# The attention stage of an audio tower on one core: the order of one group's work, by pairs of heads instead of single heads

## The chip, the cores and the metric

The kernel runs on one core of a Trainium2 chip. The metric is the device time of one execution in microseconds (us).

## The reference

The input is 32 clips of 375 frames with 80 features. A tokenizer turns windows of 8 frames (stride 4) into slots (93 a clip for the 375 frames of this input) with 256 features each (two dense layers with relu, then a batch normalisation). Then follow one attention layer and one mixture-of-experts layer:

```python
h = tok(x)                                   # (32, slots, 256)
h = h + attn(layernorm(h))                   # 16 heads of 64
h = h + ffn(layernorm(h))                    # a shared expert, and 2 of 8 routed ones
...
q, k, v = (einsum('bsm,hmd->bhsd', x, kernel[i]) for i in range(3))
attn = softmax(einsum('bhsd,bhtd->bhst', q, k) * scale, axis=-1)
out = einsum('bhst,bhtd->bhsd', attn, v)
out = transpose(out, (0, 2, 3, 1)).reshape(b, s, d * h)
out = einsum('bsf,fm->bsm', out, WO[0])
...
probs = softmax(einsum('bsh,he->bse', x, router_w)); top_k_prob, top_k_idx = top_k(probs, 2)
```

Everything is float32. The batch normalisation needs all clips before the attention starts.

## The kernel before

There are three stages, one after the other: the tokenizer, the attention with the router, and the experts. The change is in the second alone. It works on NG = 8 groups of GB = 4 clips (N = 372 token columns, C = 3 chunks of R = 124 rows). The 16 heads of a group are taken as NJ = 8 pairs j, and a head is called a unit u (NU = 16; unit u belongs to pair u // 2). The engines work through hand-written lists of steps, each list in its own order, and wait for each other through semaphores.

The steps of a pair on TensorE (PE):

- `qk_tile` "qj" and "kj": 6 matmuls each of 128x128 by 372 columns (line 908). Every product is made of three passes of high and low halves.
- `scores(g, j)`: 16 matmuls on 64 rows of the array (line 921). The two heads sit on the upper and the lower 64 rows and run side by side.
- `turn(g, u)`: 4 transposes of the unit's scaled probabilities (line 929) into the one bank t_ps.
- `values(g, j)`: 16 matmuls (line 942) that fill 64 columns of the array each. The two heads sit on different columns and run side by side.
- `output(g, j)`: 9 matmuls into y_ps (line 954).
- `v_tile`: 6 matmuls by 512 columns (line 894), 8 such tiles a group.

Between these stand the single steps of the neighbouring groups: `rows_tile` "p10" and "p11" (the next group's rows, line 626), `back_tile` "z20", "z21" (the last group's normalised rows, turned for the router) and "z10", "z11" (the next group's, turned for its projections; line 634), `logits_tile` (lines 644, 646) and `rank_tile` (lines 655, 657).

All tiles named q, k, v, p, z, logits and rank pass through two banks of pj_ps, bank 0 and bank 1, each in a fixed order. `begin` makes TensorE wait until the tile before in the same bank has been taken out. ScalarE (ACT) takes q, k, p10, p11 and the v tiles of bank 0; VectorE (DVE) takes the v tiles of bank 1, the logits and the ranks. A z tile is taken by both: ACT writes the high half (`hi`), then DVE the low half (`lo`), and only then is the bank free. k, p11 and the v tiles with an odd last digit are in bank 1, the rest in bank 0, and z tiles go by their last digit.

The chain of a unit: `scores` (PE), `shift` (DVE: maximum, line 1164, and subtraction, line 1167), `exps` (ACT, line 1063), `total` (DVE: sum, line 1173, and reciprocal, line 1175), the scaling (GpSimd, line 1301), `turn` (PE), `take_turned` (ACT, line 1069), `values` (PE), `take_o` (ACT high half, line 1074, then DVE low half, line 1179), `output` (PE). prob and probT have four slots each, u % 4.

Before, each list went over 16 slots s, one unit a slot. On TensorE an even slot held scores, both projections, an output, a v tile where the table V has one, turn(s - 2) and values, and an odd slot a v tile and turn(s - 2). So values stood between the two turns of a pair, and the odd unit's turn ahead of the next scores. DVE interleaved one shift with one total, and ran the router's steps (`route`: max, shift, sum, recip, scale, top, index, expert, masks, both, rank, pick, slots) in small portions between them. The first group has no group behind it and the last none ahead; groups 2 to 6 run in a loop with register counters. After the last group comes `drain`, and beside it the shared expert's weights are split (`shared_hi` on ACT, `shared_lo` on DVE).

Of the kernel before, what the change touches and what calls it, by code (L numbers as in the profile page):

```python
# [79 lines left out]
def audio_tower_kernel(nc, x, W1, b1, W2, b2, gamma, beta, qkv_w, WO, sh_up, sh_down, rt_up, rt_down, router_w, out):  # L80
# [8 lines left out]
    MC = HD // P  # L89
# [25 lines left out]
    with ExitStack() as ctx:  # L115
# [416 lines left out]
        with ExitStack() as c:  # L532
# [353 lines left out]
            def _(pe):  # L886
# [73 lines left out]
                def group(g, behind, ahead):  # L960
                    V = {0: "v00", 1: "v01", 2: "v02", 3: "v03", 5: "v10", 7: "v11", 9: "v12", 11: "v13"}
                    for s in range(NU):
                        if s > 0 and s % 2 == 0:
                            scores(g, s // 2)
                        if s % 2 == 0 and s // 2 + 1 < NJ:
                            qk_tile(g, "q%d" % (s // 2 + 1))
                            if s == 0:
                                scores(g, 0)
                            qk_tile(g, "k%d" % (s // 2 + 1))
                        if s % 2 == 0 and s >= 6:  # L970
                            output(g, s // 2 - 3)
                        elif s % 2 == 0 and behind:
                            output(g - 1, NJ + s // 2 - 3)
                        if s == 10 and behind:
                            logits_tile(pe, g, g - 1)
                        if s == 14 and ahead:
                            qk_tile(g, "q0")
                        if s in V:
                            v_tile(g, V[s])
                        if s == NU - 1 and behind:  # L980
                            rank_tile(pe, g, g - 1)
                        if s >= 2:
                            turn(g, s - 2)
                        elif behind:
                            turn(g - 1, NU + s - 2)
                        if s == NU - 1 and ahead:
                            qk_tile(g, "k0")
                        if s in (1, 2) and ahead:
                            rows_tile(pe, g, s - 1, g + 1)
                        if s == 9 and behind:  # L990
                            back_tile(pe, g, 1, 1, g - 1, x_rows)
                            back_tile(pe, g, 1, 0, g - 1, x_rows)
                        if s == 13 and ahead:
                            back_tile(pe, g, 0, 0, g + 1, z_rows)
                            back_tile(pe, g, 0, 1, g + 1, z_rows)
                        if s % 2 == 0 and s >= 4:
                            values(g, s // 2 - 2)
                        elif s % 2 == 0 and behind:
                            values(g - 1, NJ + s // 2 - 2)
# [18 lines left out]
                def drain():  # L1018
                    g = NG - 1
                    output(g, NJ - 3)  # L1020
# [10 lines left out]
            def _(act):  # L1031
# [44 lines left out]
                def group(g, behind, ahead):  # L1076
                    V = {0: "00", 2: "02", 5: "10", 9: "12"}
                    for s in range(NU):
                        if s % 2 == 0 and s // 2 + 1 < NJ:
# [838 lines left out]
```

## Time and profile before

| | |
|---|---|
| median of 3 runs | 1072.42 us (1072.33 to 1073.98) |
| the profiled execution, its own time | 1070.59 us |
| its span in the profile | 1069.0 us |
| TensorE matmul busy | 1018.5 us, 95% of the span |
| VectorE, ScalarE, GpSimd busy | 621.9, 507.6, 426.1 us |
| attention stage on TensorE | from 103.8 us (first scores) to 609.4 us |

The busy time of TensorE is the union of modelled intervals, so two starts in a row tell more of its pace than its busy share. In a timeline a row is a block of equal instructions: start, length, engine, line, operation, tiles, count, and in brackets the idle time ahead of it with what ended it.

### The profile page before, as it was taken

Reading aid. Unit: us, or ns where it says so; the run is one execution under the profiler, and the core shown is the slowest. Engines: PE = TensorE matmul, PEld = TensorE weight load, DVE = VectorE, ACT = ScalarE, POOL = GpSimd, SP = SyncE. Lnnn points to the kernel's source line nnn. Section 1 sums busy time; section 2 is a strip of 40 time slices with the busy share of each in tenths; the row PEclk is TensorE's granted clock in tenths of the full one; section 3 lists DMA queues with packets and bytes.
Section 4 is the critical chain, followed back from the end, with each engine's and each line's share of the span. In section 5 each row is a group of like instructions: output and inputs, shape, how many; then the busy total and the mean of one; then the engine's idle time right before and its main releaser. Section 6 shows DMA issues by size and latency. Waiting matters only on the chain. (4 is left out here: it accounts for less than half of the span.)

```text
span 1069.0 us, 24219 instructions
## 1 busy us (share of the span) xinstructions
PE 1018.5 (95%) x8364; PEld 948.6 (89%) x8365; DVE 621.9 (58%) x1610; ACT 507.6 (47%) x1129; POOL 426.1 (40%) x535
## 2 busy tenths in 40 slices
PE   5995999999999999999999799999999999999998
PEld 5994798888888888888888699999999999999998
DVE  3665666767777676877757655433443343363565
ACT  3552554444544445454444464444555454454352
POOL 2001231445253443525343250606661626543885
PEclk9997999999999999999999699999999999999999
DMA  9615999900010100001011153331443134411555
GB/s 185 140 42 196 362 345 344 330 15 17 29 29 29 24 33 14 14 29 29 29 25 45 53 158 99 103 136 60 138 137 123 58 128 133 137 51 43 163 155 137
DMA packets 104628, 115.32 MB, mean 108 GB/s; under 512 B 29856, under 2 KB 94848, under 8 KB 104576
## 3 DMA queue, kind: packets, MB, share of 16 engines
q1 hardware_dynamic: 75936, 73.82, 22.6%
q0 software_dynamic: 18176, 29.12, 9.4%
q10 hardware_dynamic: 10464, 11.70, 3.3%
q8 instruction: 31, 0.51, 0.2%
q14 instruction: 21, 0.17, 0.0%
HBM read 51.53 MB, written 62.95 MB: 107 GB/s over the span
## 5 line engine op out<-in xcount | busy, mean ns | idle before, releaser
L1301 POOL TENSOR_TENSOR prob<-prob,rc 93x372 f32<-93x372 f32 x128 | 102.9, 804 | 294.4 <-DVE rc L1175 293.9
L1856 DVE TENSOR_TENSOR act_s<-up_ps,act_s 128x384 fp32r<-128x384 f32 (+1 forms) x168 | 81.7, 493 | 176.6 <-ACT up_ps L1703 175.3
L908 PE MATMUL pj_ps<-xg,wA 128*128 128x372 f32 x768 | 151.5, 344 | 5.4 <-DVE split L744 2.7
L1701 ACT ACTIVATE act_s<-up_ps 128x384 fp32r<-128x384 f32 (+1 forms) x168 | 73.7, 439 | 148.8 <-PE up_ps L1594 144.3
L908 PEld LDWEIGHTS pj_ps<-xg,wA 128*128 128x128 f32 x768 | 128.8, 190 | 13.3 <-DVE split L744 3.8
L894 PE MATMUL pj_ps<-wB,xg 128*93 128x512 f32 x384 | 102.6, 403 | 0.8 <-ACT h_s L666 0.8
L1069 ACT ACTIVATE probT<-t_ps 93x372 f32<-93x372 f32 x128 | 60.5, 473 | 83.7 <-PE t_ps L929 83.3
L1594 PE MATMUL up_ps<-rx,wB 128*128 128x256 f32 (+1 forms) x576 | 86.4, 308 | 0.7 <-issue 0.7
L1179 DVE TENSOR_TENSOR oT<-o_ps,oT 128x372 fp32r<-128x372 f32 x64 | 34.8, 543 | 89.3 <-ACT oT L1074 88.3
L1608 PE MATMUL dn_ps<-wB,act_s 128*128 128x256 f32 x720 | 85.5, 279 | 0.0
L1594 PEld LDWEIGHTS up_ps<-rx,wB 128*128 128x128 f32 x576 | 83.6, 188 | 1.6 <-issue 0.9
L954 PE MATMUL y_ps<-wB,oT 128*124 128x256 f32 x576 | 81.7, 287 | 2.3 <-DVE oT L1179 2.3
L1608 PEld LDWEIGHTS dn_ps<-wB,act_s 128*128 128x128 f32 x720 | 83.4, 188 | 0.0
L1164 DVE TENSOR_REDUCE mx<-s_ps 93x4 f32<-93x372 f32 x128 | 67.2, 525 | 22.7 <-PE s_ps L921 22.4
L954 PEld LDWEIGHTS y_ps<-wB,oT 128*124 128x124 f32 x576 | 76.8, 189 | 3.5 <-DVE oT L1179 2.7
L894 PEld LDWEIGHTS pj_ps<-wB,xg 128*93 128x93 f32 x384 | 56.6, 158 | 25.3 <-ACT h_s L666 2.0
L1490 POOL DMA_INDIRECT raw<-y_rows,y_at x48 | 62.6, 1305 | 31.6 <-issue 31.0
L1703 ACT ACTIVATE up_ps<-up_ps 128x384 f32<-128x384 f32 (+1 forms) x168 | 71.2, 424 | 5.3
L1167 DVE TENSOR_TENSOR prob<-s_ps,mx 93x372 f32<-93x372 f32 x128 | 69.4, 542 | 7.5
L929 PEld LDWEIGHTS t_ps<-ident,prob 93*93 93x93 f32 x512 | 59.3, 163 | 16.2 <-issue 6.2
L929 PE MATMUL t_ps<-ident,prob 93*93 93x93 f32 x512 | 65.2, 250 | 4.9 <-POOL prob L1301 4.8
L1173 DVE TENSOR_REDUCE sm<-prob 93x4 f32<-93x372 f32 x128 | 67.5, 527 | 4.0 <-ACT prob L1063 4.0
(201 smaller groups left out, 1958.7 us busy)
## 6 DMA issues: line engine op xcount, KB each, us to landing
slots<-zeros SPq DMA_DIRECT2D x8, 3072.0 KB, 23.3
y_rows<-zeros SPq DMA_DIRECT2D x5, 2688.0 KB, 20.0
rows_in<-slots SPq DMA_DIRECT2D x22, 384.0 KB, 3.5
y_rows<-rows_out ACTq DMA_DIRECT2D x22, 384.0 KB, 2.5
raw<-in_L_ffn_routed_up POOLq DMA_DIRECT2D x7, 1024.0 KB, 5.4
raw<-in_L_ffn_routed_down POOLq DMA_DIRECT2D x7, 1024.0 KB, 8.2
ln_out<-split SPq DMA_DIRECT2D x8, 744.0 KB
frames<-in_x SPq DMA_DIRECT2D x8, 400.0 KB
```

What stands on the lines that cost most here:

```text
L894: ins = pe.matmul(pj_ps[0:TP, b % 2, 0:VW], xg[:, dp, m, b * TP:(b + 1) * TP], wB[:, wp, at:at + VW], start=(k == 0), stop=(k == 5))
L908: ins = pe.matmul(pj_ps[:, t, 0:N], wA[:, wp, at:at + P], xg[:, dp, m, :], start=(k == 0), stop=(k == 5))
L929: ins = pe.transpose(t_ps[:, i * TP:(i + 1) * TP], prob[:, u % 4, i, :], ident[0:TP, 0:TP])
L954: ins = pe.matmul(y_ps[0:R, c // 2, c % 2 * HD:(c % 2 + 1) * HD], oT[:, j % 2, dp, c * R:(c + 1) * R], wB[:, wp, at:at + HD], start=(j == ...
L1167: dve.tensor_tensor(prob[:, u % 4, :, 0:SL], s4, mx[:, u % 2, :].unsqueeze(2).broadcast_to([TP, 4, SL]), ALU.subtract).then_inc(shifted, 1)
L1173: dve.tensor_reduce(sm[:, u % 2, :], prob[:, u % 4, :, 0:SL], AX, ALU.add).then_inc(sum_done, 1)
L1301: pool.tensor_tensor(p, p, rc[:, u % 2, :].unsqueeze(2).broadcast_to([TP, 4, SL]), ALU.mult).then_inc(scaled, 1)
L1594: ins = pe.matmul(up_ps[:, f % 4, 0:width], w[:, wp, at:at + P], rx[:, dp, m, 0:width], start=(k == 0), stop=(k == 5))
L1608: ins = pe.matmul(dn_ps[:, a // 2, a % 2 * HD:(a % 2 + 1) * HD], act_s[:, dp, f, a * P:(a + 1) * P], w[:, wp, at:at + HD], start=(k == 0), ...
L1701: act.activation(act_s[:, HI, f, 0:width], up_ps[:, f % 4, 0:width], ACT.Gelu).then_inc(ract_hi, 1)
L1703: act.activation(up_ps[:, f % 4, 0:width], up_ps[:, f % 4, 0:width], ACT.Gelu).then_inc(rgelu_done, 1)
L1856: dve.tensor_tensor(act_s[:, LO, f, 0:width], up_ps[:, f % 4, 0:width], act_s[:, HI, f, 0:width], ALU.subtract).then_inc(ract_lo, 1)
```

## The change

Every list now goes over 8 pairs p. On TensorE a pair is: scores(p), q of the next pair, the turn of the odd unit 2p - 3, k of the next pair, output(p - 3), the v tile of slot 2p, the turn of the even unit 2p - 2, the v tile of slot 2p + 1, values(p - 2), and then straight the next pair's scores. In pair 0 q1 still stands ahead of the scores. The single steps keep their pair, with other neighbours: p11 is directly ahead of v03, z21 and z20 directly behind v12, z10 and z11 behind turn(10), rank behind q0 and turn(12). ACT follows: exps(2p) behind the first taken projection and turn, exps(2p + 1) behind k and behind the v tile of slot 2p; normalise_batch stands at the head of pair 0. DVE does both shifts, then both totals; total(15) comes inside the group; all the router's steps but the rank's stand ahead of take_o, in pair 6 too, where take_o(4) is the last. In the last group the shared weights' splitting goes by pairs, with the third portion on ACT directly ahead of the drain. No instruction is added or taken away, and no buffer changes.

Lines taken out are those of the functions printed above and are left out here, but for one.

```diff
--- before.py
+++ after.py
@@ -959,44 +959,53 @@
 
 def group(g, behind, ahead):
     V = {0: "v00", 1: "v01", 2: "v02", 3: "v03", 5: "v10", 7: "v11", 9: "v12", 11: "v13"}
...
+    for p in range(NJ):
+        if p > 0:
+            scores(g, p)
+        if p + 1 < NJ:
+            qk_tile(g, "q%d" % (p + 1))
+            if p == 0:
                 scores(g, 0)
...
+        if p >= 2:
+            turn(g, 2 * p - 3)
+        elif behind:
+            turn(g - 1, NU + 2 * p - 3)
+        if p + 1 < NJ:
+            qk_tile(g, "k%d" % (p + 1))
+        if p >= 3:
+            output(g, p - 3)
+        elif behind:
+            output(g - 1, NJ + p - 3)
+        if p == 5 and behind:
             logits_tile(pe, g, g - 1)
...
+        if p == NJ - 1 and ahead:
             qk_tile(g, "q0")
...
+        if 2 * p in V:
+            v_tile(g, V[2 * p])
+        if p >= 1:
+            turn(g, 2 * p - 2)
+        elif behind:
+            turn(g - 1, NU - 2)
+        if p == 1 and ahead:
+            rows_tile(pe, g, 1, g + 1)
+        if 2 * p + 1 in V:
+            v_tile(g, V[2 * p + 1])
+        if p == NJ - 1 and behind:
             rank_tile(pe, g, g - 1)
...
+        if p == NJ - 1 and ahead:
             qk_tile(g, "k0")
...
+        if p == 0 and ahead:
+            rows_tile(pe, g, 0, g + 1)
+        if p == 4 and behind:
             back_tile(pe, g, 1, 1, g - 1, x_rows)
             back_tile(pe, g, 1, 0, g - 1, x_rows)
...
+        if p == 6 and ahead:
             back_tile(pe, g, 0, 0, g + 1, z_rows)
             back_tile(pe, g, 0, 1, g + 1, z_rows)
...
+        if p >= 2:
+            values(g, p - 2)
+        elif behind:
+            values(g - 1, NJ + p - 2)
 
 def start():
     rows_tile(pe, -1, 0, 0)
@@ -1017,6 +1026,7 @@
 
 def drain():
     g = NG - 1
+    turn(g, NU - 3)
     output(g, NJ - 3)
     turn(g, NU - 2)
     values(g, NJ - 2)
@@ -1075,41 +1085,51 @@
 
 def group(g, behind, ahead):
     V = {0: "00", 2: "02", 5: "10", 9: "12"}
...
+    for p in range(NJ):
+        if p == 0 and ahead:
+            normalise_batch(g + 1)
+        if p + 1 < NJ:
+            take_q(g, p + 1, g)
+        if p >= 2:
+            take_turned(g, 2 * p - 3)
+        elif behind:
+            take_turned(g - 1, NU + 2 * p - 3)
+        exps(g, 2 * p)
+        if p + 1 < NJ:
+            take_k(g, p + 1, g)
+        if p == NJ - 1 and ahead:
             take_q(g, 0, g + 1)
...
+        if 2 * p in V:
+            take_v(g, "v" + V[2 * p])
+        exps(g, 2 * p + 1)
+        if p >= 1:
+            take_turned(g, 2 * p - 2)
         elif behind:
...
+            take_turned(g - 1, NU - 2)
+        if p == 1 and ahead:
+            take_rows(act, g, 1, g + 1)
+        if 2 * p + 1 in V:
+            take_v(g, "v" + V[2 * p + 1])
+        if p == NJ - 1 and ahead:
             take_k(g, 0, g + 1)
...
+        if p == 0 and ahead:
+            take_rows(act, g, 0, g + 1)
+        if p == 4 and behind:
             hi(act, g, 1, 1, g - 1)
             hi(act, g, 1, 0, g - 1)
...
+        if p == 6 and ahead:
             hi(act, g, 0, 0, g + 1)
             hi(act, g, 0, 1, g + 1)
...
+        if p >= 2:
+            take_o(g, p - 2)
+        elif behind:
+            take_o(g - 1, NJ + p - 2)
+        if p == 5 and behind:
+            exp_logits(act, g - 1)
+        if not ahead and p >= 6:
+            shared_hi(p - 6)
+    if not ahead:
+        shared_hi(2)
 
 def shared_hi(q):
 
@@ -1131,6 +1151,7 @@
 
 def drain():
     g = NG - 1
+    take_turned(g, NU - 3)
     take_turned(g, NU - 2)
     take_o(g, NJ - 2)
     shared_hi(3)
@@ -1178,69 +1199,57 @@
     dve.wait_ge(o_hi, g * NJ + (j + 1))
     dve.tensor_tensor(oT[:, j % 2, LO, :], o_ps[:, 0:N], oT[:, j % 2, HI, :], ALU.subtract).then_inc(o_lo, 1)
 
...
+def routing(n, steps):
+
+    for step in steps.split():
         route(dve, n, step)
 
 def group(g, behind, ahead):
     V = {1: "01", 3: "03", 7: "11", 11: "13"}
...
+    for p in range(NJ):
+        shift(g, 2 * p)
+        shift(g, 2 * p + 1)
+        total(g, 2 * p)
         if behind:
...
+            if p == 4:
+                normalise(dve, g, 1, g - 1, x_rows)
+            if p == 5:
+                keep(dve, g - 1, x_rows)
+                handed(dve, g)
+            if p == 6:
+                routing(g - 1, "sum recip scale top")
+        total(g, 2 * p + 1)
+        if p == 2 and behind:
+            add(g - 1)
+            moments(dve, g, 1, g - 1)
+            spread(dve, 1, g - 1)
+        if p == 1 and ahead:
+            moments(dve, g, 0, g + 1)
+            spread(dve, 0, g + 1)
+        if p == 5 and behind:
+            take_logits(dve, g, g - 1)
+            routing(g - 1, "max shift")
+        if 2 * p + 1 in V:
+            take_v(g, "v" + V[2 * p + 1])
+        if p == 5 and ahead:
+            normalise(dve, g, 0, g + 1, z_rows)
+        if p == 4 and behind:
+            for m in reversed(range(MC)):
+                lo(dve, g, 1, m, g - 1)
+        if p == 6 and ahead:
             lo(dve, g, 0, 0, g + 1)
             lo(dve, g, 0, 1, g + 1)
...
+        if p == 6 and behind:
+            routing(g - 1, "index expert masks both")
+        if p == NJ - 1 and behind:
+            take_ranks(dve, g, g - 1)
+            routing(g - 1, "pick slots")
+        if p >= 2:
+            take_o(g, p - 2)
+        elif behind:
+            take_o(g - 1, NJ + p - 2)
+        if not ahead and p >= 6:
+            shared_lo(p - 6)
 
 def shared_lo(q):
 
@@ -1281,7 +1290,6 @@
 
 def drain():
     g = NG - 1
-                    total(g, NU - 1)
     take_o(g, NJ - 2)
     shared_lo(2)
     shared_lo(3)
```

## Rows read from the trace of the kernel before

**Rows 1.** Who waited for whom, one middle group (217.4 to 280.2 us): total, times, longest.

```profile
PE pj_ps L908 <- DVE split L744: 0.4, 1, 0.4
```

**Rows 2.** Timeline of TensorE, one regular pair of a middle group.

```profile
308.37 0.90 PE L921 MATMUL s_ps<-kT,qT 64*93 64x93 f32 x16
309.20 2.30 PE L908 MATMUL pj_ps<-xg,wA 128*128 128x372 f32 x12
311.34 1.23 PE L954 MATMUL y_ps<-wB,oT 128*124 128x256 f32 x9
312.42 0.49 PE L929 MATMUL t_ps<-ident,prob 93*93 93x93 f32 x4
312.84 0.87 PE L942 MATMUL o_ps<-probT,v_rows 93*64 93x93 f32 x16
313.63 1.62 PE L894 MATMUL pj_ps<-wB,xg 128*93 128x512 f32 x6
315.09 0.49 PE L929 MATMUL t_ps<-ident,prob 93*93 93x93 f32 x4
```

**Rows 3.** Timeline of TensorE in the first group, around tile p11 (line 626).

```profile
113.12 1.54 PE L894 MATMUL pj_ps<-wB,xg 128*93 128x512 f32 x6
114.50 0.49 PE L929 MATMUL t_ps<-ident,prob 93*93 93x93 f32 x4
114.82 0.39 PE L626 MATMUL pj_ps<-ident,hs 128*124 128x128 f32 x2
115.98 1.60 PE L894 MATMUL pj_ps<-wB,xg 128*93 128x512 f32 x6 [0.77 <-ACT h_s L666]
```

**Rows 4.** Timeline of ScalarE, the same place: v02 and p11 taken.

```profile
114.69 0.59 ACT L1051 ACTIVATE v_rows<-pj_ps 93x512 f32<-93x512 f32 x1 [0.90 <-PE pj_ps L894]
...
115.55 0.38 ACT L666 ACTIVATE h_s<-pj_ps 124x256 f32<-124x256 f32 x1
```

**Rows 5.** Timeline of TensorE behind v12 (slot 9), with tiles z21 and z20 (line 634).

```profile
383.61 1.61 PE L894 MATMUL pj_ps<-wB,xg 128*93 128x512 f32 x6
...
385.38 1.06 PE L634 MATMUL pj_ps<-ident,x_rows 124*128 124x124 f32 x6
386.37 0.90 PE L921 MATMUL s_ps<-kT,qT 64*93 64x93 f32 x16
387.67 0.95 PE L908 MATMUL pj_ps<-xg,wA 128*128 128x372 f32 x4 [0.40 <-DVE split L744]
```

**Rows 6.** Timeline of TensorE from a group's rank tile into the next group: k0, then q1.

```profile
343.18 0.47 PE L657 MATMUL pj_ps<-both,ones_w 124*124 124x24 f32 x3
343.89 0.54 PE L929 MATMUL t_ps<-ident,prob 93*93 93x93 f32 x4 [0.24 <-POOL prob L1301]
344.21 1.27 PE L908 MATMUL pj_ps<-xg,wA 128*128 128x372 f32 x6
345.74 1.29 PE L908 MATMUL pj_ps<-xg,wA 128*128 128x372 f32 x6 [0.26 <-DVE next_row L821]
```

**Rows 7.** Timeline of VectorE, slots 11 to 14 of a middle group.

```profile
332.94 0.69 DVE L1151 COPY v_rows<-pj_ps 93x512 f32<-93x512 f32 x1
...
334.51 0.54 DVE L1164 TENSOR_REDUCE mx<-s_ps 93x4 f32<-93x372 f32 x1
...
335.55 0.16 DVE L778 TENSOR_REDUCE row_sum<-ex 124x3 f32<-124x24 f32 x1
...
340.91 0.16 DVE L789 COPY p_q<-tops 124x6 f32 x1
...
342.12 0.53 DVE L1173 TENSOR_REDUCE sm<-prob 93x4 f32<-93x372 f32 x1
```

**Rows 8.** Timeline of all engines, the stage's end: the last pair's scores and the last addition.

```profile
589.24 0.90 PE L921 MATMUL s_ps<-kT,qT 64*93 64x93 f32 x16
...
609.44 1.02 DVE L1158 TENSOR_TENSOR h_s<-h_s,y_ps 124x512 f32<-124x512 f32 x2 [2.37 <-PE y_ps L954]
```

**Rows 9.** Windows: per stretch, busy us (count) of PE, PEld, DVE, ACT, POOL, then granted clock.

```profile
596.00:598.00 2.00, 1.02 (x9) 0.81 (x7) 1.90 (x8) 1.65 (x3) 0.21 (x1) 0.78 0.00 0
```

More of the change, by code:

```diff
@@ L1091, in group @@
                             take_k(g, 0, g + 1)
-                        if s in (1, 2) and ahead:
-                            take_rows(act, g, s - 1, g + 1)
-                        if s == 9 and behind:
+                        if p == 0 and ahead:
+                            take_rows(act, g, 0, g + 1)
+                        if p == 4 and behind:
                             hi(act, g, 1, 1, g - 1)
                             hi(act, g, 1, 0, g - 1)
-                        if s == 13 and ahead:
+                        if p == 6 and ahead:
@@ L1098, in group @@
                             hi(act, g, 0, 0, g + 1)
                             hi(act, g, 0, 1, g + 1)
-                        exps(g, s)
-                        if s % 2 == 0 and s >= 4:
-                            take_o(g, s // 2 - 2)
-                        elif s % 2 == 0 and behind:
-                            take_o(g - 1, NJ + s // 2 - 2)
-                        if ahead:
-                            if s == 0:
-                                normalise_batch(g + 1)
-                        if behind:
-                            if s == 11:
-                                exp_logits(act, g - 1)
@@ L1111, in group @@
-                        if not ahead and s >= 13:
-                            shared_hi(s - 13)
+                        if p >= 2:
[8 more added lines that the diff above has]
+                        shared_hi(2)
@@ L1179, in take_o @@
                     dve.tensor_tensor(oT[:, j % 2, LO, :], o_ps[:, 0:N], oT[:, j % 2, HI, :], ALU.subtract).then_inc(o_lo, 1)
-                def routing(s, place, n):
-                    plan = {11: ("max", "shift", ""), 12: ("sum", "recip", "scale top"), 13: ("", "", "index expert masks both"),
-                            15: ("", "", "pick slots")}
-                    for step in plan.get(s, ("", "", ""))[place].split():
+                def routing(n, steps):
+                    for step in steps.split():
                         route(dve, n, step)
@@ L1209, in group @@
                             lo(dve, g, 0, 0, g + 1)
                             lo(dve, g, 0, 1, g + 1)
-                        if s in V:
-                            take_v(g, "v" + V[s])
-                        if behind:
-                            if s == 8:
-                                normalise(dve, g, 1, g - 1, x_rows)
-                            if s == 10:
-                                keep(dve, g - 1, x_rows)
-                        if s % 2 == 0 and s >= 4:
-                            take_o(g, s // 2 - 2)
-                        elif s % 2 == 0 and behind:
-                            take_o(g - 1, NJ + s // 2 - 2)
@@ L1242, in group @@
-                        if not ahead and s >= 14:
-                            shared_lo(s - 14)
+                        if p == 6 and behind:
[7 more added lines that the diff above has]
+                            take_o(g - 1, NJ + p - 2)
```

78 lines of the change are left out of this document (removed).

## The prediction

> **What bounds the kernel now.** I read the page first: TensorE's matmuls are busy for 95% of the span, and no other engine is above 58%. The list of waits, taken over one middle group, then says how much of TensorE's time is waiting at all. The reader is to see how short it is: the row of the z tiles, 0.4 us in a group of 62.8 us, is one of the two longest of TensorE [rows 1]. So the stage is bound by TensorE's own list, and a change of order can win only in two places: in what TensorE loses between blocks of different shape, and in the few waits. It can lose by making new waits. All three are read from the starts of blocks in the timeline of TensorE, since the busy time counts a modelled length that overlaps the next block.
>
> **Changes of shape.** Scores use half of the rows of the array for a head, values half of the columns, all else the whole. Four transposes ahead of another whole-array block take 0.32 us (114.50 to 114.82), but 0.42 ahead of values (312.42 to 312.84) [rows 2, 3]. A v tile takes 1.38 behind a projection (113.12 to 114.50) and 1.46 behind values (313.63 to 315.09) [rows 2, 3]. So entering a half-array block costs about 0.09 in the block before and, by the second pair of its matmuls starting later, some 0.05 to 0.07 within; leaving costs 0.08 within the next block and about 0.10 at the end of its own. A regular pair before changes shape four times: turn to values, values to v tile, turn to scores, scores to projection. After, values stand directly ahead of scores, and there are three changes. What that one change costs, no row shows. Bounds: 0, if two half-array blocks follow each other as if alike; 0.34, if it costs a way out and a way in (0.10 + 0.08 and 0.09 + 0.07). I take 0.17, one change, since the weights of one shape must leave for the other as at every other change, and once. That saves 0.17, less some 0.03 because a projection behind a turn starts a little later than one behind its like (an estimate: k0 takes 1.10 without its wait, where 6 of the 12 projections of [rows 2] take 1.07). Values meet scores in pairs 1 to 7 of groups 1 to 7 and pairs 3 to 7 of the first: 54 times. 54 x 0.135 = **7.3 us saved**.
>
> The Trainium skill has a rule here (TensorEngine Tiling (Array Packing), Key Properties): a change of tiling mode drains the engine, a change of tile within a mode doesn't. By it values to scores, columns halved to rows halved, is still a change of mode and costs one drain, as I took it; were it only another tile, the saving would be 7 us larger. The trace agrees so far as each change it has costs something; the new one it doesn't show.
>
> **Old waits that go.** I follow each tile that TensorE waited for into the new lists.
> - q1 of the next group waited for the rank's taking, on DVE behind two shifts. k0 starts 344.21 and q1 345.74: 1.53 for 1.10, and q1's own start costs 0.11 more. Ahead of it turn(13) started 0.71 behind a block of 0.33, 0.38 late [rows 6]. Now turn(13) is behind the next scores, and between rank and q1 stand k0 and values. About 0.9, 6 times: 5.4.
> - q6 waited for z20's low half: it starts 1.30 behind scores of 0.83, 0.47 late [rows 5]. Now values and scores are between (1.65 us, and the taking needs 1.30 from z20's end): 7 times, 3.3.
> - p10 waited for normalise_batch, now at the pair's head: 0.28 in six groups and 1.03 in the first: 2.7. In the last group turn(1) waited 0.8 for GpSimd and now stands 2 us later. z20's old wait for v12's taking is 0.19 to 0.28, 7 times: 1.4 (its successor is below). v03's, 0.3 in all.
> Together **13.9 us**.
>
> **New waits.** Times count from a pair's scores; q starts at 0.83, the odd turn 1.95, k 2.25, output 3.3, the even turn 4.4, then v tiles, values, next pair [rows 2].
> - v03 directly behind p11, same bank. The first group already has just this, since it has no values to put between: p11's two transposes need 0.22, but v03 starts at 115.98, 1.16 behind 114.82, so 0.93 of waiting [rows 3]. ScalarE takes v02 at 114.69, then a turn, then p11, done 115.93 [rows 4]. The new list puts exps(3), some 0.4, behind take_v too, so 1.33, and 0.06 for a start after standing still. Six groups at 1.39, and 0.40 more in the first: 8.7. On ScalarE, only take_o(7) is behind it, and waits for PE anyway.
> - z20 behind v12, now without a turn between. v12 is taken 2.23 us from its start (2.29 in the old place), and z20 is reached after 1.39 + 0.33: 0.51, 7 times: 3.6 [rows 5].
> - output(4) in pair 7 needs take_o(4), now DVE's last step of pair 6. DVE's list from v13, which is filled 7.6 us into pair 5 (8.28 long): copy and normalise 1.57 (332.94 to 334.51), take_o(3) 0.46, two shifts of 1.04 (334.51 to 335.55) [rows 7]. That ends at 3.4 of pair 6. Then total 0.66 (0.53 and a short step), four router steps 0.94 (estimates from the short steps of some 0.2), total 0.66, two lo of 0.46, then index to both 1.21 (340.91 to 342.12) [rows 7], take_o 0.54: ready at 8.5. Pair 6 is 6.26 long and TensorE reaches output at 1.2 of pair 7, which is 7.45. Late by 1.05 to 1.15, and 0.1 for the start. 6 x 1.2 = 7.4 (the last group's is counted with the tail). Behind that output wait q0, rank and k0; behind take_o on DVE are shift(14) and (15), which have 5 us of room.
> - rank needs q0's bank. Only turn(12), 0.33, is between now, where values were too; q0's taking comes 0.8 behind its end: 0.48, 6 times: 2.9.
> Together **22.6 us**. DMA issues on GpSimd keep their units, and those on SP wait for the z tiles' splitting, which stays in its pair; take_o(0), behind the additions and moments on DVE, is ready at 2.1 of pair 3, and its output comes at 3.3.
>
> **The tail.** From the last scores to the last addition it takes 20.2 us (589.24 to 609.44) [rows 8], and the granted clock falls on the way from 2.4 towards 1.2 GHz, to a mean of 0.78 in the stretch where TensorE is busy for 1.02 of 2 us [rows 9]; it had stood still for about 3 of the last 4 us. In the new order output(5) waits for a take_o(5) behind the last pick and slots, and comes 1.9 us later (8.3 against 6.4 from the last scores). The steps after it then run closer together. Worked through at full clock the tail would take 16.5, at half clock from output(5) on 21.5. The stillness ahead of output(5) is about as long as before (3.4 us), so I lean to the low clock: from -3.7 to +1.3, taken as **+0.5**.
>
> **The sum.** -7.3 - 13.9 + 22.6 + 0.5 = +1.9, say 2.0 us. The profiled execution's own time is 1070.59 (span 1069.0, 1.6 us around it), 1.8 below the median; against it the sum gives 1072.6, against the median 1074.4. Differences under 0.2%, 2.1 us, are about what a measurement of this kernel can't tell from none, so this stands on the border between no change and slower.
>
> **Rivals.**
> - *The change of shape is free between values and scores.* Another 0.17 at 54 places, of which the two ahead of output(4) are lost in its wait: -7, 1067.4. For it: both kinds run two heads side by side. Against it: every change in [rows 2] costs.
> - *DVE is ready for output(4).* If its list between v13 and take_o(4) takes 1.1 us less than the sum of its steps, 7.4 us go: 1067.0. Against it: my figures are starts to starts, and in the old trace those steps run without gaps.
> - *The tail keeps its clock.* -4.2 against my value: 1070.2. It decides at whether TensorE's stillness ahead of output(5) is short enough.
> - *Clearly slower: DVE falls behind one step more.* DVE's list in pairs 5 to 7 is full; each 1 us that it starts later, for instance when the shifts of pair 6 wait for turn(9) or a router step is slower than 0.2, comes out at output(4) in full, 7 times: at +0.8 each it is +6, 1080. The same price has a change of values to scores that costs 0.34 instead of 0.17. It decides from 0.3 us on.
>
> **Chances.** The forecast, new waits a little larger than what is saved, 0.55, with a range of its own from 1071.5 to 1077.5: of it 0.02 below, 0.25 within and 0.28 above. The free change 0.12, the ready DVE 0.12, both faster. The tail at full clock 0.08, within 0.2% by itself. Clearly slower 0.13. So faster 0.26, the same 0.33, slower 0.41. The range from 1067 to 1080 takes in the first faster cases at its edge and the slower one; a chance of 0.2 is left for two rivals at once.
>
> **What would show it.** Right: in a middle group's timeline scores start 0.17 behind the last of values; v03 starts 1.5 us behind p11; z20 half a us late; output(4) waits for DVE's oT, about 1 us in every group but the first; turn(13), q1 and q6 start without waits; DVE shows take_o(4) behind the router's mask sums. The group gets longer, from 62.8 to about 63.4 us. Wrong: output(4) or v03 without a wait, or a new wait of TensorE that I haven't named, above all ahead of scores or a turn; or a tail that isn't within 16 to 22 us.

## The result, and the profile after

The changed kernel takes 1076.99 us, median of 6 runs (1075.07 to 1077.60), where the kernel before took 1072.43 (1072.33 to 1073.98) in 6 runs on the same chip. The ratio is 1.0036, 95% interval 1.0026 to 1.0046, so it is slower by 3.9 us (2.8 to 4.9). The forecast was 1074.4 in a range from 1067 to 1080, with slower as the likeliest side at 0.41. The profiled execution, the fastest of the six, took 1075.07 (span 1073.5), 4.5 more than the profiled one of before.

The split of that time stands in one view: the windows of one middle group, from one rank tile to the next. The columns are the stretch and its length, the busy time and instructions of TensorE, its weight loads, VectorE, ScalarE and GpSimd, then the granted clock, the DMA share and GB/s. The kernel before:

```profile
343.06:405.89 62.83, 61.78 (x573) 53.86 (x571) 45.24 (x135) 30.36 (x69) 26.49 (x49) 1.00 0.08 24
```

and the changed kernel:

```profile
345.22:409.15 63.93, 60.80 (x570) 52.74 (x571) 47.94 (x134) 30.84 (x70) 26.39 (x49) 1.00 0.08 24
```

TensorE's busy time falls by 0.98 us a group; I put that down to the change of shape and to more closely packed blocks. Its idle time rises from 1.05 to 3.13. The group is 1.10 longer. VectorE's busy time, for the same list of instructions, rises by 2.7. Short products of 124x24 elements make 1.0 of that: in this group `scale` takes 616 ns instead of 173, and the two of `pick` take 430 each on average instead of 161.

Where TensorE stands still, its timeline in the changed kernel shows. The end of pair 6 and pair 7 of a middle group:

```profile
339.56 0.90 PE L921 MATMUL s_ps<-kT,qT 64*93 64x93 f32 x16
340.39 0.57 PE L929 MATMUL t_ps<-ident,prob 93*93 93x93 f32 x4
342.22 1.33 PE L954 MATMUL y_ps<-wB,oT 128*124 128x256 f32 x9 [1.27 <-DVE oT L1200]
...
344.41 0.49 PE L929 MATMUL t_ps<-ident,prob 93*93 93x93 f32 x4
345.22 0.28 PE L655 MATMUL pj_ps<-both,before_w 124*124 124x32 f32 x1 [0.32 <-ACT qT L1049]
...
346.86 0.87 PE L942 MATMUL o_ps<-probT,v_rows 93*64 93x93 f32 x16
347.66 1.28 PE L908 MATMUL pj_ps<-xg,wA 128*128 128x372 f32 x6
```

The output starts 1.83 behind a turn that is followed after 0.40 where nothing is waited for (e7 below): 1.43 late. Rank starts 0.81 behind the turn and not 0.33: 0.48. And q1, the last row, starts 0.80 behind values, at once: the old wait [rows 6] is gone. The tiles p11 and v03, same view:

```profile
362.77 0.39 PE L626 MATMUL pj_ps<-ident,hs 128*124 128x128 f32 x2
364.32 1.63 PE L894 MATMUL pj_ps<-wB,xg 128*93 128x512 f32 x6 [1.17 <-ACT h_s L666]
```

v03 comes 1.55 behind a tile of 0.22: 1.33 late, in all seven groups that have it, 0.40 more than in the first group of before [rows 3]. The z tiles behind v12:

```profile
386.84 0.48 PE L634 MATMUL pj_ps<-ident,x_rows 124*128 124x124 f32 x3
387.68 0.54 PE L634 MATMUL pj_ps<-ident,x_rows 124*128 124x124 f32 x3 [0.36 <-ACT v_rows L1061]
388.15 0.87 PE L942 MATMUL o_ps<-probT,v_rows 93*64 93x93 f32 x16
388.95 0.90 PE L921 MATMUL s_ps<-kT,qT 64*93 64x93 f32 x16
```

z20 starts 0.84 behind z21, which alone takes 0.32, so it is 0.52 late. The last two rows are values and the next scores, 0.80 apart. A regular pair now takes 7.04 or 6.99 us, from scores to scores, where it took 7.14 [rows 2]. Last, the tail:

```profile
592.67 0.90 PE L921 MATMUL s_ps<-kT,qT 64*93 64x93 f32 x16
...
599.23 0.57 PE L929 MATMUL t_ps<-ident,prob 93*93 93x93 f32 x4 [1.42 <-ACT probT L1079]
601.78 2.28 PE L954 MATMUL y_ps<-wB,oT 128*124 128x256 f32 x9 [1.99 <-DVE oT L1200]
```

From the last scores to the last addition (613.53, line 1179 of the changed kernel) it takes 20.9 us, where it took 20.2 [rows 8]. The last scores themselves come 3.4 us later than before.

### The profile page after: what moved, and what is told of

Read it like the earlier page. It is cut to its first block and busy times, and to the rows that moved or that the text cites. A ratio compares the mean times of both kernels' runs of the same rounds, so it can differ in the third digit from the quotient of the medians.

```text
span 1073.5 us, 24219 instructions
## 1 busy us (share of the span) xinstructions
PE 1011.0 (94%) x8364; PEld 940.5 (88%) x8365; DVE 639.7 (60%) x1610; ACT 510.5 (48%) x1129; POOL 425.8 (40%) x535
## 5 line engine op out<-in xcount | busy, mean ns | idle before, releaser
L1309 POOL TENSOR_TENSOR prob<-prob,rc 93x372 f32<-93x372 f32 x128 | 107.3, 839 | 286.0 <-DVE rc L1196 284.9
L908 PE MATMUL pj_ps<-xg,wA 128*128 128x372 f32 x768 | 163.9, 350 | 1.0 <-DVE xg L744 1.0
L1049 ACT ACTIVATE qT<-pj_ps 128x372 f32<-128x372 f32 x64 | 30.7, 480 | 88.3 <-PE pj_ps L908 88.3
L1073 ACT ACTIVATE prob<-prob 93x372 f32<-93x372 f32 x128 | 64.8, 506 | 16.3 <-DVE prob L1188 15.7
L838 POOL DMA_INDIRECT slots<-x_rows,slot_now x42 | 55.8, 1329 | 29.2 <-issue 29.2
```

The costliest lines, as they stand in the source:

```text
L908: ins = pe.matmul(pj_ps[:, t, 0:N], wA[:, wp, at:at + P], xg[:, dp, m, :], start=(k == 0), stop=(k == 5))
L1309: pool.tensor_tensor(p, p, rc[:, u % 2, :].unsqueeze(2).broadcast_to([TP, 4, SL]), ALU.mult).then_inc(scaled, 1)
```

## The experiments

The theory: the new order gains what the prediction said, and four new waits of TensorE, each the place of one tile behind another, eat more than that; each can be taken away by an exchange of neighbours. The rivals: the waits only move to the next step; VectorE is too full to be ready anywhere; or the time is lost through the clock. Differences to the changed kernel are worked out from the two ratios to before, times 1072.5 us. The interval of one ratio is 1 us to either side (2 us for e3, e6, e7 and e11), so e4 and e6 aren't told from the changed kernel by their times alone. The last column is read from the profiled executions: the time from the first scores to the last, against the changed kernel's 488.8 us. It leaves out the tail, whose clock differs from one execution to the next: with the changed kernel's order there, it took 22.2 us from the last scores to the next stage in the changed kernel and 20.3 (e5) to 23.5 (e1) in the others.

| | median us | ratio to before (95%) | against the changed kernel | trace, first to last scores |
|---|---|---|---|---|
| changed kernel | 1076.99 | 1.0036 (1.0026 to 1.0046) | | (before: +3.3) |
| e1_take_o_first | 1071.37 | 0.9993 (0.9983 to 1.0003) | -4.6 | -6.4 |
| e2_p11_ahead | 1071.01 | 0.9985 (0.9976 to 0.9995) | -5.5 | -6.1 |
| e3_values_between | 1079.27 | 1.0063 (1.0045 to 1.0081) | +2.9 | +2.7 |
| e4_exps_behind | 1074.78 | 1.0026 (1.0016 to 1.0035) | -1.1 | -2.8 |
| e5_v12_ahead | 1070.77 | 0.9988 (0.9978 to 0.9998) | -5.1 | -4.3 |
| e6_values_ahead_rank | 1074.91 | 1.0026 (1.0008 to 1.0045) | -1.1 | +2.5 |
| e7_all_waits | 1048.76 | 0.9774 (0.9755 to 0.9793) | -28.1 | -25.1 |
| e8_scale_early | 1074.09 | 1.0016 (1.0006 to 1.0025) | -2.1 | -2.2 |
| e9_tail | 1071.05 | 0.9986 (0.9976 to 0.9995) | -5.4 | 0.0 |
| e10_before_normalise | 1070.13 | 0.9976 (0.9967 to 0.9986) | (before: -2.6) | (before: -2.8) |
| e11_turn_between | 1056.46 | 0.9858 (0.9839 to 0.9878) | (e7: +9.0) | (e7: +10.0) |

**e1_take_o_first: output(4)'s wait.** On VectorE, pair 6, take_o goes ahead of four router steps.

```diff
-            if p == 6 and behind:
-                routing(g - 1, "index expert masks both")
             if p >= 2:
                 take_o(g, p - 2)
             elif behind:
                 take_o(g - 1, NJ + p - 2)
+            if p == 6 and behind:
+                routing(g - 1, "index expert masks both")
```

> Against the changed kernel (1077.0 us), VectorE takes o of pair 4 ahead of the four router steps index to both, in pair 6, and does nothing else otherwise. Theory: output(4) waits 1.43 us a group because those 1.21 us of steps stand ahead of take_o(4), behind a list that is full since v13; without them the wait is under 0.2, the rank's masks are still in time, and 6 groups give 7 to 8 us: about 1069. Rival: the wait is ScalarE's high half of o or the scores' shifts, and the order on VectorE doesn't matter: 1077, the wait stays over 1 us.

Measured: 1071.37. Timeline of TensorE, same place:

```profile
340.20 1.34 PE L954 MATMUL y_ps<-wB,oT 128*124 128x256 f32 x9
...
342.40 0.49 PE L929 MATMUL t_ps<-ident,prob 93*93 93x93 f32 x4
343.35 0.28 PE L655 MATMUL pj_ps<-both,before_w 124*124 124x32 f32 x1 [0.45 <-ACT qT L1049]
...
594.48 0.94 PE L929 MATMUL t_ps<-ident,prob 93*93 93x93 f32 x4 [2.85 <-ACT probT L1079]
```

The output's wait is gone but for 0.2. A middle group is 62.86, 1.07 less, and the last rank tile comes 6.2 us earlier (590.24 against 596.43; 7.5 counted from the first scores of either). The step behind the output takes 0.13 a group back, rank's own wait being 0.62 instead of 0.49. From the last rank tile to the next stage 2.4 more are lost: the turn behind that tile's values now waits 2.85 for ScalarE where it waited 1.42, and the granted clock is low from 592.9 on, where it was low from 600.8. Which of the two is the cause of the other is not shown. The place is shown, and so is that a microsecond won there isn't wholly won at the end.

**e8_scale_early: why that wait was 0.3 longer than forecast.** The router's first four steps stand ahead of both totals instead of between them.

```diff
             shift(g, 2 * p + 1)
+            if p == 6 and behind:
+                routing(g - 1, "sum recip scale top")
             total(g, 2 * p)
             if behind:
...
-                if p == 6:
-                    routing(g - 1, "sum recip scale top")
             total(g, 2 * p + 1)
```

> Against the changed kernel, the four router steps sum, recip, scale and top stand ahead of both totals in pair 6 instead of between them. The same work, 0.94 to 1.4 us, stays ahead of take_o(4). In the changed kernel scale takes 0.61 us and runs beside GpSimd's scaling of unit 12, in the kernel before 0.17 and beside nothing. Theory: scale is held up while GpSimd works, and here it takes 0.17 again, so that output(4) waits 0.44 less, 6 x 0.44 = 2.6: about 1074.4. Rival: its length comes from something else (the operands, the record); it stays 0.61 and the time 1077.

The reason for it is in the timeline of GpSimd and VectorE of the changed kernel, pair 6:

```profile
337.63 0.80 POOL L1309 TENSOR_TENSOR prob<-prob,rc 93x372 f32<-93x372 f32 x1 [5.96 <-DVE rc L1196]
337.65 0.18 DVE L780 RECIPROCAL row_sum<-row_sum 124x3 f32<-124x3 f32 x1
337.86 0.61 DVE L782 TENSOR_TENSOR ex<-ex,row_sum 124x24 f32<-124x24 f32 x1
338.63 0.30 DVE L786 MAX8 tops<-ex 124x8 f32<-124x8 f32 x3 [0.15 <-DVE ex L782]
```

The `scale` step, a product of 124x24 elements, starts 0.23 behind the start of GpSimd's scaling and ends 0.04 behind its end (338.47 and 338.43). Its median over the eight groups is 615 ns, in the kernel before 173. The reciprocal one row up, which has one input, also ran beside GpSimd and took its usual 0.18. The experiment, same step and then the output that waits:

```profile
337.45 0.18 DVE L782 TENSOR_TENSOR ex<-ex,row_sum 124x24 f32<-124x24 f32 x1
...
342.21 1.33 PE L954 MATMUL y_ps<-wB,oT 128*124 128x256 f32 x9 [0.90 <-DVE oT L1200]
```

The wait falls from 1.27 to 0.90 and the group by 0.36; 1074.09, 2.1 less, where 2.6 was expected. So total(12), by starting GpSimd, held up `scale`, which stood behind it on VectorE. The Trainium skill (SBUF — State Buffer, Who interferes with whom) has the rule: a VectorE instruction with two inputs in SBUF contends with a GpSimd instruction that reads SBUF, and the second to start is blocked until the first is done. The trace agrees to 0.04 us at the end of `scale`; whether it was held from its first element isn't shown, and spans on GpSimd are rough.

**e2_p11_ahead and e4_exps_behind: v03's wait.** e2 moves p11 (and its taking on ScalarE) from directly ahead of v03 to ahead of v02. e4 leaves TensorE alone and moves exps(3) on ScalarE from ahead of p11's taking to behind it.

```diff
 # e2, TensorE; ScalarE's take_rows likewise
+            if p == 1 and ahead:
+                rows_tile(pe, g, 1, g + 1)
             if 2 * p in V:
                 v_tile(g, V[2 * p])
...
-            if p == 1 and ahead:
-                rows_tile(pe, g, 1, g + 1)
 # e4, ScalarE
-            exps(g, 2 * p + 1)
+            if p != 1:
+                exps(g, 2 * p + 1)
...
             if p == 1 and ahead:
                 take_rows(act, g, 1, g + 1)
+            if p == 1:
+                exps(g, 2 * p + 1)
```

> Against the changed kernel, tile p11 and its taking stand ahead of v02 instead of ahead of v03; no bank order changes. Theory: v03's wait of 1.33 us in seven groups is the chain take v02, exps, take turned, take p11 on ScalarE, and goes entirely; p11 itself finds k2 taken. 7 x 1.4 = 9.5 us: about 1067.5. Rival: bank 1 is then short between k2 and p11 and the wait moves ahead by half: 1072.

> Against the changed kernel (1077.0 us), exps(3) stands behind the taking of p11 on ScalarE instead of ahead of it, so that the chain v02, turn, p11 is what it was in the kernel before. Theory: v03's wait of 1.33 us falls to the 0.93 that the first group had before; 0.4 in seven groups, 2.8 us: about 1074.2. Rival: the wait is set by v02's taking alone and stays 1.33: 1077.

e2 gives 1071.01, 5.5 less where 9.5 was expected (6.1 in the trace). v03's wait is gone (pair 1 is 8.60 long, not 10.02), but k3 has one that was not there:

```profile
302.06 0.49 PE L929 MATMUL t_ps<-ident,prob 93*93 93x93 f32 x4
302.79 1.29 PE L908 MATMUL pj_ps<-xg,wA 128*128 128x372 f32 x6 [0.24 <-DVE v_rows L1172]
```

It starts 0.73 behind the turn instead of 0.28. It needs v03's bank, and VectorE takes v03 only behind `moments` and `spread`. The group is 0.93 shorter: 1.33 less 0.45, within 0.05. Here the rival of the moved wait is right, for a third of the gain. In e4 v03 is still late, but less:

```profile
361.48 0.39 PE L626 MATMUL pj_ps<-ident,hs 128*124 128x128 f32 x2
362.64 1.63 PE L894 MATMUL pj_ps<-wB,xg 128*93 128x512 f32 x6 [0.77 <-ACT h_s L666]
```

0.77 of idle time for 1.17: the exponential's 0.40, as the prediction had put it into this wait. The group is 63.54, 0.39 less. The time is 1.1 less by the ratios and 2.2 by the medians, where 2.8 was expected; the trace up to the last scores is 2.8 shorter.

**e5_v12_ahead: z20's wait.** v12, and its taking on ScalarE, go ahead of output(1) in pair 4.

```diff
+            if p == 4:
+                v_tile(g, V[9])
             if p >= 3:
                 output(g, p - 3)
...
-            if 2 * p + 1 in V:
+            if 2 * p + 1 in V and p != 4:
                 v_tile(g, V[2 * p + 1])
```

> Against the changed kernel (1077.0 us), v12 stands ahead of output(1) in pair 4, so that an output and a turn lie between it and z21, z20. Theory: z20 waits 0.52 us in seven groups for ScalarE's taking of v12 alone, and this goes: 3.6 us, about 1073.4. Rival: z20 waits for the z21 half's taking or for the normalised rows, and stays: 1077.

```profile
383.14 1.54 PE L894 MATMUL pj_ps<-wB,xg 128*93 128x512 f32 x6
384.51 1.24 PE L954 MATMUL y_ps<-wB,oT 128*124 128x256 f32 x9
385.59 0.49 PE L929 MATMUL t_ps<-ident,prob 93*93 93x93 f32 x4
385.92 0.80 PE L634 MATMUL pj_ps<-ident,x_rows 124*128 124x124 f32 x6
```

The six transposes of both z tiles stand in one block: no wait. The group is 0.59 shorter for a wait of 0.52. Up to the last scores the trace is 4.3 shorter. The time is 5.1 less, 1.5 more than expected; in the profiled execution the clock was also low for less of the tail, which took 20.3 us to the next stage instead of 22.2.

**e6_values_ahead_rank: rank's wait.** values(5) goes ahead of rank in pair 7.

```diff
+            if p == NJ - 1:
+                values(g, p - 2)
             if p == NJ - 1 and behind:
                 rank_tile(pe, g, g - 1)
...
-            if p >= 2:
+            if 2 <= p < NJ - 1:
                 values(g, p - 2)
+            elif p >= 2:
+                pass
```

> Against the changed kernel, values of pair 5 stand ahead of the rank tile in pair 7, and k0 behind it. No meeting of values and scores is lost, since q1 follows either way. Theory: the rank's wait of 0.49 us for q0's taking goes and q1 finds the ranks taken, 6 x 0.49 = 2.9 us: about 1074.1. Rival: VectorE takes the ranks too late for q1, which is now only k0 behind, and the wait comes back as in the kernel before: 1077.

1074.91, but with runs from 1071.37 to 1079.82, far more apart than those of the others. The profiled one is the slowest. In it the one group between rank tiles in which the clock stays takes 63.35, 0.58 less than 63.93 for a wait of 0.49. In four groups it takes 64.87 to 64.89. There the windows and the timeline of TensorE show:

```profile
340.00:344.50 4.50, 3.73 (x16) 3.73 (x17) 3.28 (x9) 0.52 (x2) 0.80 (x1) 0.62 0.00 0
```

```profile
338.92 0.57 PE L929 MATMUL t_ps<-ident,prob 93*93 93x93 f32 x4
340.77 2.12 PE L954 MATMUL y_ps<-wB,oT 128*124 128x256 f32 x9 [1.28 <-DVE oT L1204]
342.69 1.97 PE L908 MATMUL pj_ps<-xg,wA 128*128 128x372 f32 x6
```

Behind the wait for take_o(4), 1.28 us of idle time, output takes 2.12 us and the projection 1.97, where they took 1.33 and 1.18. The granted clock is 0.62 over these 4.5 us, between its levels of 1.2 and 2.4 GHz, and that costs 1.5. So the exchange takes the rank's wait away, and a wait that was left standing beside it became dearer. By its times alone e6 shows no clear gain.

**e9_tail: the order in the last group.** VectorE's first portion of the shared weights goes behind the last shifts, totals and ranks, take_o(5) ahead of the ranks, and ScalarE's third portion behind the first turn of the drain.

```diff
 # VectorE
+            if p == NJ - 1 and not ahead:
+                take_o(g, p - 2)
             if p == NJ - 1 and behind:
                 take_ranks(dve, g, g - 1)
                 routing(g - 1, "pick slots")
-            if p >= 2:
+            if p == NJ - 1 and not ahead:
+                shared_lo(0)
+            elif p >= 2:
                 take_o(g, p - 2)
...
-            if not ahead and p >= 6:
-                shared_lo(p - 6)
+            if p == NJ - 1 and not ahead:
+                shared_lo(1)
 # ScalarE
-    if not ahead:
-        shared_hi(2)
...
     take_turned(g, NU - 3)
+    shared_hi(2)
     take_turned(g, NU - 2)
```

> Against the changed kernel, in the last group alone: VectorE's splitting of the shared weights' first quarter stands behind the last shifts and sums, its take_o of pair 5 ahead of the ranks, and ScalarE's third quarter behind a turn in the drain. Theory: output(5) comes some 2 us earlier, TensorE stands still less ahead of it, and the stage's end moves by 2 to 5 us, the more the later the clock falls: about 1073.5. Rival: the end is set by the last unit's chain from its scores on, whatever stands ahead: 1077.

1071.05, 5.4 less. The windows of the tail, changed kernel:

```profile
600.00:612.00 12.00, 8.93 (x58) 7.80 (x58) 5.97 (x11) 4.55 (x8) 0.57 (x1) 0.57 0.01 1
```

and e9, with the output that waits:

```profile
600.00:612.00 12.00, 8.53 (x79) 7.66 (x78) 9.26 (x20) 6.39 (x11) 1.61 (x2) 1.00 0.16 56
```

```profile
598.87 1.33 PE L954 MATMUL y_ps<-wB,oT 128*124 128x256 f32 x9 [0.38 <-DVE oT L1199]
```

output(5) starts 6.4 us behind the last scores instead of 9.1, and the granted clock is 1.00 through the whole tail, where from 600 to 612 it was 0.57. The next stage begins at 608.75 instead of 614.87, so the window of e9 has 3.25 us of it, and its counts don't compare with those of the changed kernel. The clock isn't safe in this order: in the profile of e7 (below), whose tail has it too, the first turn of the drain waits 1.34 us for ScalarE instead of 0.29, the granted clock then falls to 0.50, and from the last scores to the next stage it takes 20.5 us (568.05 to 588.58) instead of 16.3.

**e3_values_between: what values ahead of scores is worth.** The changed kernel with values ahead of the v tile in pairs 2 and 3, which takes the direct meeting away at two places of a group.

```diff
+            if p in (2, 3):
+                values(g, p - 2)
             if 2 * p + 1 in V:
                 v_tile(g, V[2 * p + 1])
...
-            if p >= 2:
+            if p >= 4:
                 values(g, p - 2)
+            elif p >= 2:
+                pass
```

> Against the changed kernel, values stand ahead of the v tile in pairs 2 and 3 of each group, so that they don't meet the scores there: 16 places with four changes of shape again instead of three. Theory: a change of shape costs some 0.17 us wherever it is, so each of these pairs is 0.14 to 0.17 us longer: 2.2 to 2.7 us, about 1079.4. Rivals: the meeting of values and scores saves nothing and only the order of waits counts: 1077.0, pairs as long as before; or the change costs 0.34: 5.4 more, 1082.

```profile
372.46 0.87 PE L942 MATMUL o_ps<-probT,v_rows 93*64 93x93 f32 x16
373.26 1.63 PE L894 MATMUL pj_ps<-wB,xg 128*93 128x512 f32 x6
374.82 0.90 PE L921 MATMUL s_ps<-kT,qT 64*93 64x93 f32 x16
```

The pair is 7.19 long instead of 7.04 and the group 0.33 longer: 0.165 a place. The time is 2.9 longer, the trace up to the last scores 2.7.

**e7_all_waits: all of them together.** e1, e2, e5, e6, e8 and e9 in one kernel, and the taking of v03 on VectorE ahead of `moments`, against the wait that e2 had uncovered.

```diff
+            if p == 1:
+                take_v(g, "v03")
             if p == 1 and ahead:
                 moments(dve, g, 0, g + 1)
...
-            if 2 * p + 1 in V:
+            if 2 * p + 1 in V and p != 1:
                 take_v(g, "v" + V[2 * p + 1])
```

> All together on the changed kernel: p11 ahead of v02 (with v03 taken ahead of the moments on VectorE, which in the run with p11 ahead alone had left 0.40 us of waiting at k3), v12 ahead of output(1), values ahead of the rank, take_o(4) ahead of index to both, scale ahead of the totals, and the tail's order. Theory: the new waits are all that was wrong with the change, they add up, and the gain of three changes of shape instead of four and of the old waits stays: 3.8 us less a middle group (60.2 against 63.9), 22.6 for six, 2 in the first and last, 3 in the tail: about 1050, faster than both kernels. Rival: with the waits gone VectorE, busy for most of a group, is the next bound, and half comes back as waits for it: 1062.

1048.76 us, ratio 0.9774 to before. Its windows for one middle group, and pair 7 in the timeline of TensorE:

```profile
334.14:394.10 59.96, 59.96 (x572) 52.86 (x570) 46.83 (x135) 30.72 (x70) 26.32 (x48) 1.00 0.09 26
```

```profile
329.51 0.90 PE L921 MATMUL s_ps<-kT,qT 64*93 64x93 f32 x16
330.34 0.57 PE L929 MATMUL t_ps<-ident,prob 93*93 93x93 f32 x4
330.74 1.32 PE L954 MATMUL y_ps<-wB,oT 128*124 128x256 f32 x9
...
333.35 0.87 PE L942 MATMUL o_ps<-probT,v_rows 93*64 93x93 f32 x16
334.14 0.28 PE L655 MATMUL pj_ps<-both,before_w 124*124 124x32 f32 x1
```

TensorE is busy for 59.96 of 59.96 us. The steps that waited for 1.43 and 0.49 stand without a gap. The rival that VectorE is too full falls with this: it does the same work, 46.83 us of it, and is in time everywhere.

**e11_turn_between: the gain of the order itself.** e7 with the even unit's turn, and its taking, behind values in pairs 0 to 6, so that values no longer meet scores, at 54 places.

```diff
-            if p >= 1:
+            if p == NJ - 1:
                 turn(g, 2 * p - 2)
...
             elif behind:
                 values(g - 1, NJ + p - 2)
+            if 1 <= p < NJ - 1:
+                turn(g, 2 * p - 2)
+            elif p == 0 and behind:
+                turn(g - 1, NU - 2)
```

> Against the version with all waits mended (1048.8 us), the even unit's turn, and its taking on ScalarE, stand behind values instead of ahead of them, in pairs 0 to 6. So values and scores meet nowhere any more, 54 places, and nothing else of the order changes. Theory: each place costs one change of shape, 0.165 us: 8.9 us, about 1057.7; a middle group goes from 59.96 to some 61.1. Rival: the meeting is worth little, and the mended version is fast for its waits alone: 1049 to 1051. Other rival: the turn is now too near the next pair's odd turn, through ScalarE and the one bank, and TensorE waits there: over 1062.

```profile
332.45 0.87 PE L942 MATMUL o_ps<-probT,v_rows 93*64 93x93 f32 x16
333.25 0.57 PE L929 MATMUL t_ps<-ident,prob 93*93 93x93 f32 x4
333.74 0.90 PE L921 MATMUL s_ps<-kT,qT 64*93 64x93 f32 x16
...
376.79 1.23 PE L954 MATMUL y_ps<-wB,oT 128*124 128x256 f32 x9
378.14 0.85 PE L634 MATMUL pj_ps<-ident,x_rows 124*128 124x124 f32 x6
```

1056.46: 9.0 us more than e7 by the ratios, 7.7 by the medians. Up to the last scores the trace is 10.0 longer (473.7 against 463.7), and the tail is shorter, with a higher clock. The group is 1.38 longer. In the first rows the turn takes 0.49 up to the scores, where it takes 0.28 between two whole-array blocks. The last two rows show that not all of it is the change of shape: z21 starts 1.35 behind the output, where it starts 1.08 behind it in the second group, which has no wait there. It waits for the normalised rows, which VectorE finishes at 378.01, and no longer has a turn ahead of it. TensorE stands still ahead of z21 for 1.8 us in six groups together. Without that 8.2 us are left, 0.15 a place.

**e10_before_normalise: one old wait.** The kernel before, with only normalise_batch moved to the head of ScalarE's group.

```diff
 # ScalarE, kernel before
+    if ahead:
+        normalise_batch(g + 1)
     for s in range(NU):
```

> The kernel before (1072.4 us) with one part of the change alone: ScalarE's normalise_batch at the head of a group instead of at the end of its first slot. Theory: p10's wait goes, 1.03 us in the first group and 0.28 in six: 2.7 us, about 1069.7. Rival: the two instructions, 1.27 us, now hold up q1 and k1 and with them the next scores, and it comes out the same: 1072.4.

1070.13, 2.6 less than before for an expected 2.7. In the first group p10 has no idle time ahead of it, where it had 0.88:

```profile
109.31 0.60 PE L626 MATMUL pj_ps<-ident,hs 128*124 128x128 f32 x4
```

The middle group is 62.52, 0.31 less. This is a gain of the change that doesn't need its order.

## Why the prediction was right

**The change of shape** (-7.3). Taken as one change of 0.17 between values and scores, so that 0.135 a place is saved. The two regular pairs show it directly, 7.04 and 6.99 for 7.14: 0.10 and 0.15. Taken back, it costs 0.165 a place in e3 and 0.15 in e11. With the free change 0.3 a place would be saved, with the dear one nothing, so both rivals fall.

**The old waits** (-13.9). None of turn(13), q1, q6, p10 and turn(1) waits any longer. e10 prices one of them by itself, p10's, 2.6 for 2.7. The others are priced with the change of shape together: for a middle group the prediction's terms are 0.95 for seven changes of shape and 0.9, 0.47, 0.28, some 0.2 for z20 and 0.04 for v03, in all 2.84. e7, which has all of these gains and none of the new waits, has a group 2.87 shorter than before (59.96 and 62.83).

**The new waits** (+22.6). All four are where they were said, and the list of TensorE's waits over a middle group names no other: v03 1.33 (forecast 1.33 and 0.06 for the start), z20 0.52 (0.51), rank 0.49 (0.48). The term that was mis-sized is output(4): 1.43, where 1.05 to 1.15 and 0.1 for the start had been forecast, so 8.6 us instead of 7.4. The step is "four router steps 0.94": it priced them by short steps that ran alone, but the new order puts them behind a total, which starts GpSimd, and one took 0.61 instead of 0.17. e8 shows it. The rival "clearly slower" had named a slower router step, at +0.8; it came at +0.2 to +0.3.

**The tail** (+0.5). To the first matmul of the next stage it takes 22.2 us (592.67 to 614.87) instead of 21.5 (589.24 to 610.78), so +0.7. The clock fell as before, and TensorE stood still for 3.4 us ahead of output(5), as forecast. That the term came out so close is partly luck: output(5) came 9.1 us behind the last scores and not 8.3, and against that the clock was up again before the last output, which took 1.32 instead of 2.28. The five other runs of the changed kernel, with mean clocks of 0.981 to 0.986 for this one's 0.987, took 1.2 to 2.5 us longer; how their tails went isn't traced. e9 shows that another order can keep the clock: 16.3 us to the next stage (from 592.50), a gain of 5.9 on the changed kernel. e7 shows that this order doesn't always, and what decides it isn't settled.

**The sum.** +1.9 was forecast. With what was measured for the new waits (23.5) and the tail it is -7.3 - 13.9 + 23.5 + 0.7 = +3.0. The ratio says +3.9 (2.8 to 4.9), the profiles +4.5, of which 4.0 are in the attention stage. About 1.0 of what is beyond lies ahead of the tail: from the first scores to the last it takes 488.8 us instead of 485.5, 3.3 more, and without the tail the terms make 2.3.

In a middle group it is 0.17 (the waits of 1.33, 0.52, 1.43 and 0.49 less 2.84 make +0.93, and it is 1.10 longer). Set beside the pairs of e7, which have no waits, it sits in the three pairs with the new waits, each of which is longer by more than its waits: pair 1 by 1.41 for 1.33, pair 4 by 0.59 for 0.52, pair 7 by 1.99 for 1.92. All other pairs are as long as in e7. So some 0.07 more is lost wherever TensorE had to wait, and no wait is missing from the list. The prediction had such a term for the start after standing still, 0.06 at v03 and 0.1 at the output, and none at z20 and rank. The rows don't say what the 0.07 is made of.

With these starts and the output's wait both taken too small, the group was forecast at about 63.4 us and came to 63.93, and the forecast loss of 2.0 us is half of the measured one. The places, their order and the direction were right, the size was not.

**What the whole change was worth.** With the new waits mended and another order in the tail, the same arrangement gains 24.2 us on the kernel before (e7). That it came out slower is no fault of values ahead of scores; some 8 of those us are their own (e11). Not all of the 24.2 needs the new order: the 2.6 of e10 don't, and the tail's new order wasn't tried in the kernel before.

## What to carry to other kernels

Where the longest queue has no gaps left, price a new order tile by tile: for each bank or buffer, what stands between its two users now, and whether that covers the taking. A wait that such a list foretells is mostly mended by the exchange of two neighbours, but do it until nothing stands still, as each mended wait may uncover a shorter one (k3 here). Compare the starts of blocks for that: z21's wait of some 0.3 in e11 is hidden behind the modelled length of the block before it. A short VectorE step is not cheap wherever it stands: a product of two SBUF tensors, placed behind the step that starts GpSimd, lasted as long here as GpSimd's product did.

## What the runs showed of the hardware that was not expected

- A VectorE product of 124x24 took 0.61 us beside GpSimd's scaling and 0.17 to 0.18 alone.
- TensorE's clock can fall in the midst of a busy stretch. In e6 the granted clock was 0.62 over the 4.5 us around a wait of 1.28 us, between the levels of 1.2 and 2.4 GHz, and the work behind the wait took 1.5 us longer. Four groups of that execution are longer by as much; a wait of 1.27 in the changed kernel's profile had no such effect (granted clock 1.00 through the group). What made the difference is open.
- Column halves directly ahead of row halves, with no whole-array block between, save 0.10 to 0.165 us a place. That is about one of the two changes of shape, which the prediction estimated at 0.17 each, so going from halves to halves costs about as much as going from whole array to halves.
